# First and middle stage of a three-stage kernel in one program: memory handed over in place, the first items prepared within the last batch

## What is computed

```python
x = x + attn(cond(x, ..., adapter_ids), w_qkv, b_qkv, w_dense, b_dense)      # first stage
h = cond2(x, Wq, Wk, Wv, Wo, q_norm_w, k_norm_w, k_cache, v_cache, block_table, cache_seqlens)
x = x + ffn(h, W, b, A, B, gate_w, gate_b)                                   # last stage

# cond2 (middle stage)
q, k, v = x @ Wq.T, x @ Wk.T, x @ Wv.T          # heads of 128: 32, 8, 8
q, k = rope(rmsnorm(q) * q_norm_w, pos), rope(rmsnorm(k) * k_norm_w, pos)
k_all = concat(k_cache[block_table], k); v_all = concat(v_cache[block_table], v)   # 512 + 128 positions
probs = softmax(where(valid, q @ k_all.T / sqrt(128), -1e30))
h = (probs @ v_all) @ Wo
```

## Time and profile before

| what | value |
|---|---|
| median of 3 runs | 1420.65 us (1418.09 to 1422.16) |
| profiled execution | 1419.12 us, of which the span from first to last instruction 1417.3 us |
| TensorE busy | 1356.8 us (96%) |
| VectorE busy | 1092.3 us (77%) |
| ScalarE busy | 860.1 us (61%) |
| POOL busy | 655.3 us (46%) |
| chain that ended last | TensorE holds 77% of the span |
| granted TensorE clock, mean | 0.989 of full speed |

### The profile page before, as it was taken

One profiled execution on the slowest core, in us unless ns is written; L12 is line 12 of the kernel. 1 busy time (PEld: TensorE's weight loads), 2 busy tenths in 40 slices (PEclk: granted clock), 3 DMA queues, 4 the chain that ended last, 5 costly groups with the idle time before them and its releaser, 6 DMA issues.

```text
span 1417.3 us, 26026 instructions
## 1 busy us (share of the span) xinstructions
PE 1356.8 (96%) x7832; PEld 1141.4 (81%) x7832; DVE 1092.3 (77%) x2968; ACT 860.1 (61%) x2499; POOL 655.3 (46%) x652
## 2 busy tenths in 40 slices
PE   4999998679999999999999999999999999999988
PEld 3655665368888888888888888888888888888877
DVE  3787787458888888888888888887888888888855
ACT  1556666446666666667666766676666666666631
POOL 1344554445365446545453635364436544554511
PEclk9999999899999999999999999999999999999999
DMA  7444444442212222121213121212131221212121
...
DMA packets 193518, 107.56 MB, mean 76 GB/s; under 512 B 140897, under 2 KB 178274, under 8 KB 191970
## 3 DMA queue, kind: packets, MB, share of 16 engines
...
q10 hardware_dynamic: 1154, 0.50, 0.1%
...
## 4 chain that ended last, share of the span: by engine, by line
PE 77%; DVE 2%; ACT 1%; issue 0%; POOL 0%; DVEq 0%; ACTq 0%; POOLq 0%
PE b_ps L1072 11%; PE b_ps L1074 11%; PE b_ps L1073 11%; PE b_ps L1121 10%; PE b_ps L1142 5%; PE b_ps L1136 5%; PE b_ps L1135 5%; PE b_ps L1153 4%; PE b_ps L1152 4%; PE b_ps L1159 4%; PE b_ps L1097 2%; PE b_ps L796 1%; PE b_ps L795 1%; PE b_ps L794 1%; PE b_ps L1102 0%
## 5 line engine op out<-in xcount | busy, mean ns | idle before, releaser
L1265 ACT ACTIVATE b_pf<-b_sm,b_nb,b_rstd 128x640 f32<-128x640 f32 x256 | 235.0, 918 | 103.4 <-DVE b_nb L1370 103.1
L1271 ACT ACTIVATE b_p_h<-b_ps 128x640 fp32r<-128x640 f32 x256 | 180.3, 704 | 178.6 <-PE b_ps L1121 178.0
L1384 DVE TENSOR_TENSOR b_p_l<-b_ps,b_p_h 128x640 fp32r<-128x640 f32 x256 | 210.5, 822 | 77.7 <-ACT b_p_h L1271 69.8
L1363 DVE CUSTOM_DVE_ANT_0 b_sm<-b_ps,mask_row 128x640 f32<-128x640 f32 x256 | 208.9, 816 | 2.0 <-PE b_ps L1074 1.7
L1121 PE MATMUL b_ps<-ident,b_pf 128*128 128x128 f32 x1280 | 181.6, 273 | 7.8 <-DVE b_p_l L1384 5.2
L1072 PE MATMUL b_ps<-w_h,x1t_h 128*128 128x512 f32 (+1 forms) x512 | 179.4, 350 | 7.7 <-POOL w_l L1452 6.3
L1379 DVE TENSOR_SCALAR b_pf<-b_pf,b_ri 128x640 f32<-128x640 f32 x256 | 159.7, 624 | 27.7 <-DVE b_ri L1376 0.5
L1072 PE MATMUL b_ps<-b_kt_h,b_qt_h 128*128 128x320 f32 x512 | 174.1, 340 | 2.0 <-DVE b_mx L1363 1.2
L1074 PE MATMUL b_ps<-w_h,x1t_l 128*128 128x512 f32 (+1 forms) x512 | 173.9, 340 | 0.0
L1121 PEld LDWEIGHTS b_ps<-ident,b_pf 128*128 128x128 f32 x1280 | 151.7, 140 | 27.1 <-issue 6.8
L1073 PE MATMUL b_ps<-w_l,x1t_h 128*128 128x512 f32 (+1 forms) x512 | 173.4, 339 | 0.0
...
## 6 DMA issues: line engine op xcount, KB each, us to landing
kv_of_batch<-in_kv SPq DMA_DIRECT2D x128, 256.0 KB
...
b_cv<-kv_of_batch SPq DMA_DIRECT2D x256, 64.0 KB, 2.2
...
```

The source lines that it names most:

```text
L1265: act.activation(pf[:, h % 2], sm[:, h % 2], ACT.Exp, bias=nb[:, m.b % 2, h:h + 1], scale=rstd[:, m.b % 4, h:h + 1], accum_out=rs[:, m.b % ...
L1271: act.activation(p_h[:, :, h * P:(h + 1) * P], turned_row, ACT.Copy).then_inc(ph_sb, 1)
L1363: dve.tensor_tensor_reduce(sm[:, h % 2], score_row, mask_row[:, m.b], 1.0, MASKED, ALU.add, ALU.max, mx[:, k, h:h + 1]).then_inc(mx_sb, 1)
L1384: dve.tensor_tensor(p_l[:, :, cols], turned_row, p_h[:, :, cols], ALU.subtract).then_inc(pl_sb, 1)
```

## The change

Both stages run in one block. `phase1` no longer opens one; it returns its five streams as functions (`run_sync`, `run_tensor`, `run_scalar`, `run_vector`, `run_gpsimd`), and each stream of `phase2` calls its own first. PSUM is allocated once for both. The SBUF tensors of `phase1` are still freed at its end and those of `phase2` placed over them, in an order of declarations that lays each new tensor over one which is read for the last time earlier. The two short slots are gone; their parts are passed to `phase1` as functions (`ahead`) and are called within slots 6, 7 and 8. `hacc` is a tensor of `phase2`, no longer cleared: the first head group copies into it.

```diff
+LAST = B - 1
 # SyncE, slot(b) of phase1
                 if inside(b - 2):
                     store(b - 2)
+                if b == LAST:
+                    sp.wait_ge(gathered, 16 * EARLY * B)
+                    cache_rows(Item(0, 0))
+                if b == LAST + 1:
+                    sp.wait_ge(gathered, 16 * EARLY * (B + 1))
+                    cache_rows(Item(0, 1))
+                    first_out_weights()
                 if inside(b):
                     load_in(b)
...
             store(B - 1)
-            sp.wait_ge(gathered, 16 * EARLY * (B + 1))
-            sp.wait_ge(x1_out, 16 * B)
 # TensorE
+                if b == LAST + 1:
+                    pe.wait_ge(masked, 8 * B)
+                    next_scores(Item(0, 0), 0)
...
                 if inside(b + 1):
                     project_q(b + 1)
+                if b == LAST:
+                    pe.wait_ge(qt_sb, B)
+                    project_next_q(Item(0, 0))
                 if inside(b):
                     scores(b, 4)
                 if inside(b - 1):
                     context(b - 1, 1)
                 if inside(b + 1):
                     project_kv(b + 1)
+                if b == LAST:
+                    pe.wait_ge(bd_sb, KT * B)
+                    project_next_kv(Item(0, 0))
                 if inside(b):
                     scores(b, 5)
...
+                if b == LAST:
+                    turn_next_q(Item(0, 0))
                 if inside(b - 1):
                     turn_x1(b - 1)
                 if inside(b):
                     context(b, 0)
+                if b == LAST:
+                    turn_next_k(Item(0, 0))
+                    project_next_q(Item(0, 1))
+                if b == LAST + 1:
+                    project_next_kv(Item(0, 1))
 # ScalarE
+                if b == LAST + 1:
+                    next_cache_values(Item(0, 0))
...
                     exponent(b, 5)
+                if b == LAST:
+                    next_squares(Item(0, 0))
+                if inside(b):
                     exponent(b, 6)
+                if b == LAST:
+                    next_kv(Item(0, 0))
...
                     exponent(b, 7)
+                if b == LAST:
+                    next_queries(Item(0, 0))
+                    next_cache_keys(Item(0, 0))
+                    next_keys(Item(0, 0))
...
                     probs_out(b, 5)
+                if b == LAST - 1:
+                    next_weights()
+                if b == LAST:
+                    next_squares(Item(0, 1))
 # VectorE
+                if b == LAST + 1:
+                    next_maxima(Item(0, 0), 0)
+                    next_products(Item(0, 1))
...
                     probs_out(b, 2)
+                if b == LAST:
+                    next_products(Item(0, 0))
...
                     residual(b - 1)
+                if b == LAST:
+                    next_values(Item(0, 0))
...
                     mask(b + 1, 0)
+                if b == LAST:
+                    next_queries(Item(0, 0))
                 if inside(b):
                     invert(b, 7)
+                if b == LAST:
+                    next_keys(Item(0, 0))
 # POOL
                     normalize(b, 2)
+                if b == LAST:
+                    next_kv_weights(0)
...
                     normalize(b, 4)
+                if b == LAST:
+                    next_queries(Item(0, 0))
+                if inside(b):
                     with_bias(b)
                     normalize(b, 5)
+                if b == LAST:
+                    next_rms(Item(0, 0))
+                    next_keys(Item(0, 0))
+                if inside(b):
                     normalize(b, 6)
                     normalize(b, 7)
+                if b == LAST - 1:
+                    next_q_weights(0, range(KT))
+                if b == LAST:
+                    next_cache_keys(Item(0, 0))
+                    next_cache_values(Item(0, 0))
+                    next_queries(Item(0, 1))
 # phase2, slots
-            zero, one = Item(0, 0), Item(0, 1)
-            slot(None, None, zero, None)
-            slot(None, zero, one, None)
 # phase2, SyncE: the last 11 gathers
-                if two and two.g == 0 and two.b < 4:
-                    first = EARLY * (B + 1)
-                    for n in range(first + 3 * two.b, min(first + 3 * (two.b + 1), B * NPP)):
+                if two and two.g == 0 and two.b in (2, 3, 4, 5):
+                    first = EARLY * (B + 1) + 3 * (two.b - 2)
+                    for n in range(first, min(first + 3, B * NPP)):
                         gather(sp, t, pages, kv_dram, gathered, n)
 # phase2, TensorE: project and out_of_highs wait for x1t_l in the first head group
+                if m.g == 0:
+                    pe.wait_ge(xl_sb, m.b + 1)
...
+                if m.n == 0:
+                    pe.wait_ge(xl_sb, B)
 # phase2, VectorE
                 dve.wait_ge(wo_ps, m.n + 1)
+                if m.g == 0:
+                    dve.tensor_copy(hacc[:, m.b], ps[:, SM, :]).then_inc(h_sb, 1)
+                    return
                 dve.tensor_tensor(hacc[:, m.b], ps[:, SM, :], hacc[:, m.b], ALU.add).then_inc(h_sb, 1)
...
-            dve.memset(hacc[:], 0.0).then_inc(const_sb, 1)
-            dve.wait_ge(const_sb, 2)
+            vector_first(dve, (rope_products, new_values, queries, new_keys, maxima))
```

141 lines of the change are left out of this document (71 added, 70 removed).

## The result

| kernel | median (runs) | profiled execution | its span | mean clock |
|---|---|---|---|---|
| before | 1420.65 us (1417.61 to 1422.16, 5) | 1419.12 us | 1417.3 us | 0.989 |
| after | 1414.95 us (1413.41 to 1416.39, 5) | 1414.67 us | 1412.9 us | 0.991 |

The ratio is 0.9965 with a 95% interval of 0.9953 to 0.9976: faster by 5.7 us of the medians, 0.35%. Ten further runs gave 1415.5 against 1419.57 us and the same 0.9965. Forecast were 1410.4 us and a gain of 10.3. The time lies in the range, but the gain is about half.

The account below looks back on a forecast made before the run. TensorE bounds the kernel except at the seam between first and middle stage: 24.6 us saved, 15.6 paid in slot 7, drain 2.7 shorter to 0.2 longer, middle gain 10.3; 1420.65 - 10.3 = 1410.4 us, range 1402 to 1417.

Parts of the forecast that it names:

- The price in slot 7 and the drain: Last batch's slot pays 15.6 us; drain 2.7 us shorter to 0.2 longer; against 24.6 saved, gain 8.8 to 11.7.
- the turning: TensorE's turning of item (0,1)'s queries, starting the first regular middle-stage slot: forecast at 288.5 or 291.4 us.
- the last turning: TensorE's last transposition of probabilities in the first stage: forecast at 278.5 us, 15.6 us late.
- upper-clock case: Drain after the last batch, with TensorE at the upper clock: 8.5 us, against 11.4 at the lower.
- 300.18: Start in us of the first regular middle-stage slot in the old trace, against which the forecast start was set.
- From then on TensorE sets the pace in every slot, and the gain is kept to the end: Behind the first regular slot's start: distance to the end unchanged at 1117.1 us.
- The memset goes too; it is hidden now and its loss brings nothing: VectorE's clearing of the running sum, beside the weight split: removing it is worth nothing.
- The barrier itself is thus cheap (under 0.5 us): Between first and middle stage: engines start the next program within 0.5 us; the 24.8 us of serial steps cost.
- (a): Slot 7: preparation disappears into gaps, total delay 8 instead of 15.6 us, gain 16 to 19, about 1403; chance 0.13.
- (b): Lower clock holds from the second projection through slot 7: gain 4.8 or 2.8 us; chance 0.18 together with (d).
- (c): SyncE's two waits for page gathers, x = 3 us each assumed, make it slower; gain gone at 9.4; chance 0.05.
- (d): Memory handed over early makes someone wait, so no overlap: 1416 to 1420 us; chance 0.18 together with (b).

Follow-up runs that it names:

- e1: Kernel before with only the middle stage's SBUF tensors declared in the changed kernel's order, still two programs: 1423.5 us, ratio 1.0017.
- e3: Kernel before with only the 20-byte `half` declared ahead of the tables, shifting tables, running sum and split weights by 32 bytes: 1422.5 us, ratio 1.0018.
- e8: Changed kernel with 32 unused bytes ahead of the split weights and 32 behind, putting the weights on a multiple of 64 bytes: 1411.9 us, ratio 0.9948.
- e5: Changed kernel with VectorE's one-column bias written with one tensor input instead of two: 1413.8 us, ratio 0.9963.
- e7: Changed kernel without the spreading: one program, all preparation of items (0,0) and (0,1) behind the last batch again; median 1418.8 us, ratio 0.9991.
- e11: The kernel of e7, unchanged, in another profiled execution: shared median 1418.8 us, ratio 0.9991.
- e13: Kernel before, two programs, with the running sum no longer cleared; the first head group copies into it: 1418.5 us, ratio 0.9980.
- e2: Changed kernel with the weight splits moved earlier, into POOL's gaps in slot 6 and right behind slot 7's first normalization: 1405.7 us, ratio 0.9899.

## Why the prediction was half right

- **The price in slot 7 and the drain**: right. Forecast was a gain of 8.8 to 11.7; the lead at the turning is 9.6 us in the first pair of profiles, and the seam is 8.8 us shorter on average. The projections ran mostly at the lower clock (4.5, 2.7 and 4.6 us instead of 3.0, 2.4 and 3.0), which made the last turning 2.4 us later than forecast; the drain with the last projection took 9.7 us from there, the 10.0 of the forecast's upper-clock case (8.5 + 1.5): dense product (3.70) and context ran at that clock. That the total fits is in part luck: a turning 2.4 us late was met by the shorter of the two drains, and the 300.18 that it was set against moves with the store's landing and the clock (seams of 87.9 to 90.6).
- **"From then on TensorE sets the pace in every slot, and the gain is kept to the end"**: this step failed. It was taken for granted since the diff moves no instruction there. But it moves tensors: 1.6 us by the weights' address (shown: e1, e3, e8), and instructions against one another by nanoseconds: 0.84 and 1.19 us at a lock (shown: e5). In the prediction's terms, the loss behind the seam stood at nothing, and it was 5.2 us. The last 1.5 us of it, the clock in the last slot, can't be put down to the change: the last part took 82.2 to 83.0 us in nine of the 18 profiles of the table and 83.7 to 84.5 in the others, both with either order of tensors, and one kernel had both (e7 and e11). That before was short and after long in both their profiles is then chance, or a matter of how often, which 18 profiles don't tell. The 0.84 at the first lock isn't in every execution either (e11).
- **"The memset goes too; it is hidden now and its loss brings nothing"**: wrong (e13). It did not falsify the sum, because the sum took away the whole stretch in which it stood. But it falsifies the reading that only the serial steps cost: one edit of the kernel before had 4.4 of the seam's 8.8 us in its profile, 2.3 of them surely its own.
- **"The barrier itself is thus cheap (under 0.5 us)"**: true of the one execution that was read, where the drain was slow. In the three other profiles of kernels with two programs that clear the sum it was 2.8, 3.5 and 4.4 us, set by the landing of x1's last store. Joining and not clearing are 7.2 of the 8.8 us by the profiles, and the spreading over slot 7, with all its payments, brings the rest; by the medians the spreading brings more.
- **Rivals.** (a), the preparation disappears in gaps, was not so in after, for the reason given against it, and is nearly what e2 makes of it by using exactly POOL's gaps. (b), the lower clock, came for the projections and not for the dense products. (c): SyncE's two waits took 246.18 - 242.14 = 4.0 and 279.93 - 275.56 = 4.4 us (x = 3 was assumed), far under 9.4, and nobody waited. (d): no wait of that kind.
